# Expert token lists built in three groups instead of two, and expert 0's first layer run between the last group's sums

## The reference

```python
route_prob = jax.nn.softmax(xf @ Ws + bs, axis=-1).T
route_vals, routes = jax.lax.top_k(route_prob, k)      # E = 8 experts, k = 512 tokens each
xin = xf[routes]
h = jax.nn.gelu(jnp.einsum('ekd,edf->ekf', xin, W1) + b1[:, None, :])     # D = 256, F = 1024
out = jnp.einsum('ekf,efd->ekd', h, W2) + b2[:, None, :]
out = out * route_vals[..., None]
final = jnp.zeros((N, D)).at[routes.reshape(-1)].add(out.reshape(-1, D))
```

## Time and profile before

| what | us |
|---|---|
| median of 3 runs | 802.96 |
| lowest, highest | 799.78, 806.54 |
| span of the profiled execution (first to last instruction) | 760.2 |
| TensorE busy in the span | 695.7 |
| VectorE busy | 501.5 |
| ScalarE busy | 348.2 |
| GpSimd busy | 247.4 |

### The profile page before, as it was taken

One profiled execution on the slowest core, in us unless ns is written; L12 is line 12 of the kernel. 1 busy time (PEld: TensorE's weight loads), 2 busy tenths in 40 slices (PEclk: granted clock), 3 DMA queues, 4 the chain that ended last, 5 costly groups with the idle time before them and its releaser, 6 DMA issues.

```text
span 760.2 us, 25608 instructions
## 1 busy us (share of the span) xinstructions
PE 695.7 (92%) x11058; PEld 618.6 (81%) x11058; DVE 501.5 (66%) x1159; ACT 348.2 (46%) x765; POOL 247.4 (33%) x358
## 2 busy tenths in 40 slices
PE   7998998999989999999999999508999999999993
PEld 6886787989978999899899888407689998999992
DVE  6716774555446678777767677678378878877820
ACT  2663544445544546655656564530353345325410
POOL 5510044555644413223140431001734253203333
PEclk9998999999999999999999998755899999999997
DMA  7960024343443635454544453720735255312213
GB/s 201 391 276 2 31 99 153 109 135 124 157 149 112 196 96 158 135 165 140 168 109 142 138 164 108 262 49 3 233 130 154 54 156 139 120 21 28 29 21 36
DMA packets 75467, 96.81 MB, mean 127 GB/s; under 512 B 11337, under 2 KB 67057, under 8 KB 74202
## 3 DMA queue, kind: packets, MB, share of 16 engines
q1 hardware_dynamic: 62250, 69.52, 28.0%
q0 software_dynamic: 12288, 25.12, 13.2%
q10 hardware_dynamic: 816, 0.53, 0.2%
HBM read 53.78 MB, written 41.55 MB: 125 GB/s over the span
## 4 chain that ended last, share of the span: by engine, by line
PE 78%; DVE 10%; issue 4%; DMA 3%; POOL 2%; ACT 1%; POOLq 0%; DVEq 0%
PE bank L1828 41%; PE attn L1828 27%; PE bank L1786 3%; PE bank L1880 2%; DVE arena L1488 2%; PE bank L1887 1%; DMA arena<-x_p,idxs 1%; PE attn L2189 1%; DMA big<-o_m,gidx 1%; DVE st L1043 1%; PE attn L1771 1%; PE attn L1990 1%; POOL arena L524 1%; POOL big L467 1%; DVE big L1056 1%
## 5 line engine op out<-in xcount | busy, mean ns | idle before, releaser
L1828 PE MATMUL attn<-arena 32*32 32x64 f32 (+4 forms) x6048 | 140.3, 225 | 9.2 <-issue 7.3
L1828 PE MATMUL bank<-xT,arena 128*128 128x128 f32 (+2 forms) x964 | 145.8, 306 | 0.0
L1828 PEld LDWEIGHTS attn<-arena 32*32 32x32 f32 (+3 forms) x6048 | 114.2, 120 | 33.2 <-issue 15.4
L1828 PEld LDWEIGHTS bank<-xT,arena 128*128 128x128 f32 x964 | 124.3, 192 | 11.2 <-issue 5.8
L467 POOL DMA_INDIRECT big<-o_m,gidx x64 | 71.0, 1109 | 159.7 <-PE bank L1828 116.9
L460 POOL DMA_INDIRECT x_c<-big,sidx x64 | 68.6, 1071 | 119.3 <-PE bank L1828 88.9
L1828 PE MATMUL bank<-arena,xT 128*128 128x128 f32 (+2 forms) x640 | 107.1, 320 | 0.1
L1828 PEld LDWEIGHTS bank<-arena,xT 128*128 128x128 f32 x640 | 90.0, 199 | 8.6 <-issue 2.9
L543 POOL DMA_INDIRECT out_dram<-arena,idxs x32 | 50.2, 1569 | 109.6 <-ACT arena L1010 99.3
L1165 DVE COPY_PREDICATED arena<-causal,attn 128x1024 f32<-128x1024 int32 x24 | 31.6, 1316 | 71.2 <-PE attn L1828 71.2
L524 POOL DMA_INDIRECT arena<-x_p,idxs x32 | 34.3, 1070 | 98.8 <-DVE idxs L1567 70.8
(11 more groups left out here) (305 smaller groups left out, 1249.2 us busy)
## 6 DMA issues: line engine op xcount, KB each, us to landing
x_c<-zeros SPq DMA_DIRECT2D x8, 1024.0 KB, 9.2
xT<-x_c SPq DMA_DIRECT2D x16, 512.0 KB, 4.1
o_m<-arena SPq DMA_DIRECT2D x16, 512.0 KB, 4.0
xT<-in_L_ffn_W_dram SPq DMA_DIRECT2D x8, 1024.0 KB, 7.9
gs<-in_L_ffn_W_dram SPq DMA_DIRECT2D x8, 1024.0 KB, 7.6
xT<-in_L_attn_x_dram SPq DMA_DIRECT2D x8, 512.0 KB, 5.2
out_dram<-xT SPq DMA_DIRECT2D x8, 512.0 KB, 5.2
arena<-in_L_attn_x_dram SPq DMA_DIRECT2D x7, 512.0 KB, 6.2
```

The costliest lines, as they stand in the source:

```text
L1828: return nc.tensor.matmul(out_, l, r, start=a, stop=z, skip_group_check=True)
```

## The change

The groups become expert 0 alone, experts 1 to 3, and experts 4 to 7. `one_hots` is split, so that the low digit's code of the next group is written before VectorE turns to the wait for the sums of the group before (`low_hots`). The list sums use bank 3, bank 2 and bank 3. Expert 0's blocks move from banks 2 to 5 to banks 4 to 7. The two halves of the last group's sums, and its `spread`, move into `first_hidden`, between the halves of expert 0's layer 1. SP's weights of experts 2 and 3 wait for the last list sum (`s_idx`) and no longer for the turned rows. `warm(14)` and `warm(8)` stand around the second group's sums; the fill-in of 8 behind the last sum goes, and the one of 6 becomes 4. The instructions of POOL are the same as before; `gather(1)` now waits for the second list.

The diff:

```diff
--- before.py
+++ after.py
@@ -34,7 +34,8 @@
 GATED = 1360.0
 E, F = 8, 1024
 HI, LO = 32, 16
-LISTS = ((0, 4), (4, 8))
+LISTS = ((0, 1), (1, 4), (4, 8))
+LIST_BANK = (3, 2, 3)
 NL = len(LISTS)
 PARTS = ((0, NT - 2), (NT - 2, NT))
 EG = max(hi - lo for lo, hi in LISTS)
@@ -666,7 +667,7 @@
 
             def load_w(e):
                 if e == 2:
-                    sp.wait_ge(e_tp, 2)
+                    sp.wait_ge(s_idx, NL)
                 if e >= NW:
                     sp.wait_ge(y_p, 7 * (e - NW + 1))
                 sp.dma_start(w1s[e % NW], W1[e].rearrange("(k p) f -> p k f", p=P)).then_inc(e_w[e % NW], 16)
@@ -968,7 +969,7 @@
             def first_slot():
                 for f in range(FT):
                     act.wait_ge(e_h, f + 1)
-                    nc.scalar.activation(ht[:, 0, f, :], bank[2 + f % 4][:, :], ACT.Gelu_apprx_tanh,
+                    nc.scalar.activation(ht[:, 0, f, :], bank[4 + f % 4][:, :], ACT.Gelu_apprx_tanh,
                                          bias=b1c[:, f:f + 1]).then_inc(e_gl, 1)
                     if f == 2:
                         rows_t(1, 1)
@@ -1545,11 +1546,15 @@
             def over_c(a, lo, hi, n, at):
                 return et(a)[:, lo:hi, at].unsqueeze(2).to_broadcast([P, hi - lo, n, NT // 2])
 
-            def one_hots(q, h):
+            def low_hots(q, h):
                 lo, hi = LISTS[q]
                 at = slice(NT // 2 * h, NT // 2 * h + NT // 2)
                 nc.vector.tensor_tensor(ohb[:, lo:hi, :, at], over_c(digit_f[:, 1, :], lo, hi, LO, at),
                                         over_e(number[:, 0:LO, at], hi - lo), ALU.is_equal).then_inc(s_low, 1)
+
+            def one_hots(q, h):
+                lo, hi = LISTS[q]
+                at = slice(NT // 2 * h, NT // 2 * h + NT // 2)
                 nc.vector.tensor_tensor(oha[:, lo:hi, :, at], over_c(digit_f[:, 0, :], lo, hi, HI, at),
                                         over_e(number[:, :, at], hi - lo), ALU.is_equal)
                 dve.wait_ge(s_low, 2 * q + h + 1)
@@ -1559,7 +1564,8 @@
             def by_digits(q):
                 n = LISTS[q][1] - LISTS[q][0]
                 dve.wait_ge(s_idx, q + 1)
-                nc.vector.tensor_copy(cidx[0:n * HI, q, 0:n * LO], bank[3 + q][0:n * HI, 0:n * LO]).then_inc(s_idxc, 1)
+                nc.vector.tensor_copy(cidx[0:n * HI, q, 0:n * LO], bank[LIST_BANK[q]][0:n * HI, 0:n * LO])\
+                    .then_inc(s_idxc, 1)
 
             def token_list(q):
                 lo, hi = LISTS[q]
@@ -1567,14 +1573,23 @@
                 nc.vector.tensor_scalar(idxs[:, lo:hi, :], attn[:, 0:hi - lo, 8 * q:8 * q + JT], float(B * S // 2),
                                         None, ALU.add).then_inc(s_list, 1)
 
-            for q in range(NL):
-                for h in range(2):
-                    one_hots(q, h)
-                    if q and h == 0:
-                        by_digits(q - 1)
-                        token_list(q - 1)
-            by_digits(NL - 1)
-            token_list(NL - 1)
+            for h in range(2):
+                low_hots(0, h)
+                one_hots(0, h)
+            low_hots(1, 0)
+            by_digits(0)
+            token_list(0)
+            one_hots(1, 0)
+            low_hots(1, 1)
+            one_hots(1, 1)
+            low_hots(2, 0)
+            by_digits(1)
+            token_list(1)
+            one_hots(2, 0)
+            low_hots(2, 1)
+            one_hots(2, 1)
+            by_digits(2)
+            token_list(2)
 
 
             def gate_column(e):
@@ -2155,7 +2170,7 @@
                 n = hi - lo
                 pe.wait_ge(s_oh, 2 * q + h + 1)
                 for t in range(NT // 2 * h, NT // 2 * h + NT // 2):
-                    ins = mm(bank[3 + q][0:n * HI, 0:n * LO], oha[:, lo:hi, :, t].rearrange("p e c -> p (e c)"),
+                    ins = mm(bank[LIST_BANK[q]][0:n * HI, 0:n * LO], oha[:, lo:hi, :, t].rearrange("p e c -> p (e c)"),
                              ohb[:, lo:hi, :, t].rearrange("p e c -> p (e c)"), t == 0, t == NT - 1)
                 if h:
                     ins.then_inc(s_idx, 1)
@@ -2173,10 +2188,10 @@
             by_lists(0, 0)
             by_lists(0, 1)
             spread(0)
+            warm(14, bank[5])
             by_lists(1, 0)
-            warm(5, bank[7])
+            warm(8, bank[5])
             by_lists(1, 1)
-            warm(8, bank[7])
 
             def rows_t(e):
                 pe.wait_ge(e_x[e % 3], 16 * JT * (e // 3 + (e % 3 > 0)))
@@ -2201,7 +2216,7 @@
             def hidden_half(f, h):
                 t = slice(KTOP // 2 * h, KTOP // 2 * h + KTOP // 2)
                 for k in range(2):
-                    ins = mm(bank[2 + f][:, t], w1s[0][:, k, P * f:P * f + P], xet[:, 0, k, t], k == 0, k == 1)
+                    ins = mm(bank[4 + f][:, t], w1s[0][:, k, P * f:P * f + P], xet[:, 0, k, t], k == 0, k == 1)
                 if h:
                     ins.then_inc(e_h, 1)
 
@@ -2209,22 +2224,26 @@
                 pe.wait_ge(e_w[0], 32)
                 first_rows_t(0)
                 spread(1)
-                warm(6, bank[5])
-                pe.wait_ge(s_list, NL)
+                warm(4, bank[5])
                 pe.wait_ge(e_xt, 1)
                 hidden_half(0, 0)
                 hidden_half(1, 0)
+                by_lists(2, 0)
                 first_rows_t(1)
                 hidden_half(2, 0)
+                by_lists(2, 1)
+                pe.wait_ge(e_xt, 2)
                 hidden_half(3, 0)
-                pe.wait_ge(e_xt, 2)
-                for f in range(4):
+                hidden_half(0, 1)
+                spread(2)
+                for f in range(1, 4):
                     hidden_half(f, 1)
+                pe.wait_ge(s_list, NL)
                 rows_t(1)
                 for f in range(4, FT):
                     pe.wait_ge(e_gl, f - 3)
                     for k in range(2):
-                        ins = mm(bank[2 + f % 4][:, :], w1s[0][:, k, P * f:P * f + P], xet[:, 0, k, :], k == 0, k == 1)
+                        ins = mm(bank[4 + f % 4][:, :], w1s[0][:, k, P * f:P * f + P], xet[:, 0, k, :], k == 0, k == 1)
                     ins.then_inc(e_h, 1)
 
             def hidden_product(n, k, w, x, first=True):
@@ -2251,13 +2270,9 @@
                 hidden_product(n, 1, w1sum[:, 2, :], xsum[:, 2, :])
                 if n:
                     pe.wait_ge(h_c, 3 * n)
-                else:
-                    pe.wait_ge(e_gl, 5)
                 hidden_product(n, 2, w1sum[:, 0, :], xsum[:, 0, :])
                 pe.wait_ge(h_u, 2 * n + 1)
                 hidden_product(n, 0, w1_part(e, 0, 1), x_part(e, 1, 0), False)
-                if n == 0:
-                    pe.wait_ge(e_gl, 6)
                 hidden_product(n, 3, w1_part(e, 1, 1), xsum[:, 3, :])
                 pe.wait_ge(h_c, 3 * n + 1)
                 hidden_product(n, 2, w1sum[:, 3, :], x_part(e, 1, 1), False)
```

## The result

| | median us | lowest, highest | runs |
|---|---|---|---|
| before | 799.76 | 792.39, 806.54 | 20 |
| after | 794.41 | 791.82, 800.09 | 20 |

The ratio is 0.9946, with a 95% interval of 0.9928 to 0.9965: a gain of about half a per cent, within 1% as forecast, but with an interval that does not hold 1, where I had said "no shift". The forecast was set on the median of 3 runs, 802.96, and that lies 3.2 us above the median of 20; the other 5.35 us of the miss are the change.

A forecast was written before the change was run, and what follows sets the result against it. The start of hidden(0) was taken to bound the kernel, with expert 1's gather only 1.1 us late. The steps summed to expert 1's turning at 546.4 against 546.40, no shift: 803.0 us, range 799.0 to 808.0.

The forecast's parts named there:

- no shift: Main case: expert 1's turning stays at 546.4 against 546.40, so the time stays 803.0; chance 0.35.
- step 7: Expert 0's first blocks start 1.95 us after the turning, at 533.5; the pair takes 3.03, to 536.5.
- Steps 1 and 2: List 0's codes are ready at 522.2; its 32 sums start at 522.75, take 1.6 us, end at 524.35.
- Steps 3 and 4: Index tile 0 comes at 525.3, 3.4 us earlier; POOL starts at 526.2; expert 0's rows are turned from 531.55.
- step 4: Expert 0's first rows land 4.95 us after the first issue, plus 0.4 for busy VectorE; turning starts at 531.55.
- Step 5: List 1's sums run from 526.7 to near 530.7, ahead of the first turning at 531.55; tile 1 at 533.45.
- Step 6: Expert 1's gather waits for tile 1 until 534.3, lands near 541.3 instead of 546.36; SP's weights start after it.
- Steps 7 and 8: Expert 0's blocks start at 533.5, with list 2's halves of 1.98 us in between; expert 1's turning at 546.4.
- The clock falls in the list sums: Rival: list 2's sums between the blocks keep TensorE at half clock, up to 4.5 us; 805.5, worst 807.5; chance 0.3.
- Small products cost as much as large ones: Rival: list 0's sums take 4.3 us, moving all later steps by 2.7, to 805.7; chance 0.1.
- GpSimd is held up: Rival: GpSimd's first issue waits for VectorE's codes until 529.0, first rows 1.7 us later, 804.7; chance 0.1.
- A gain: Rival: clock up before the first blocks (1.3), list 0's sums 0.4 us (1.2), no overlap cost (0.4); 800.1; chance 0.15.

The follow-up runs named there:

- b_again: The kernel before, unchanged, run and profiled again at the upper level: 799.27 us, ratio 0.9995 to the kernel before.
- a_again2: The changed kernel, unchanged, run a third time, at the lower level: 766.47 us, ratio 1.0026 to the kernel before.
- a_wide: The changed kernel with the second group's products over experts 0 to 3 (128 weight columns, not 96): 763.04 us, ratio 0.9999 to the kernel before.
- b_gather_late: The kernel before with expert 1's gather waiting for the last list: 768.06 us, ratio 1.0046 to the kernel before.
- b_banks4: Fourth run of the kernel before with expert 0's blocks in banks 4 to 7 and the s_list wait behind them: 764.31 us, ratio 0.9991.
- b_banks: The kernel before with expert 0's blocks in banks 4 to 7 and the s_list wait behind them: 763.89 us, ratio 1.0001.
- b_banks2: Second run of the kernel before with expert 0's blocks in banks 4 to 7 and the s_list wait behind them: 764.96 us, ratio 1.0019.
- b_banks3: Third run of the kernel before with expert 0's blocks in banks 4 to 7 and the s_list wait behind them: 763.29 us, ratio 0.9993.
- b_banks_wait_kept: The kernel before with expert 0's blocks in banks 4 to 7 but the s_list wait left ahead of them: 764.65 us, ratio 0.9993.
- b_banks_tile_late: b_banks with VectorE writing the last index tile only after expert 1's rows landed: 764.38 us, ratio 0.9980 to the kernel before.
- b_tile_late: The kernel before with VectorE writing the last index tile only after expert 1's rows landed: 769.36 us, ratio 1.0082.
- b_weights_late: The kernel before with SP's weights of experts 2 and 3 waiting until expert 1's rows are turned: 799.19 us, ratio 0.9991.
- a_again: The changed kernel, unchanged, run again at the upper level: 794.35 us, ratio 0.9926 to the kernel before.
- a_sums_ahead: The changed kernel with both halves of the last list's sums ahead of expert 0's blocks: 797.48 us, ratio 0.9974 to the kernel before.

## Why the prediction was wrong, point by point

**What bounds the kernel now.** "Whatever moves the start of `hidden(0)` moves the end": right. From there to the end of the span are 205.94 to 206.10 us in 19 of the 20 profiles, and 206.80 in b_again. What failed is what follows it: that the gather is late by 1.1 us and that this is all that can be given back, and with it step 7, which lets the blocks start 1.95 us after the turning before the change as well as after it. Both are true of the execution that I read and not of the runs that were timed. There the kernel before starts its blocks 7.18 us after the turning, 5.05 of them idle in the wait `s_list` for the last index tile, and the change, which has this wait behind the blocks, starts them 1.76 after it. So the term that the sum puts at nothing without a reason is the wait `s_list`. What hid it is the step from the profiled span to the median: 42.8 us between them is more than 5% of the time, and I wrote it off.

**Steps 1 and 2, list 0.** The sums start when the 40 fill-ins end, as said, but the fill-ins are not fixed at 3.87 us: they took 3.09 in the profile after, and the sums start 1.19 us after the first code where 2.1 were forecast. The sums take 1.99 for 32 products of 32x16: 0.062 each, 1.6 forecast, within its bounds. The Trainium skill (TensorE: Matmul & The Clock Gate, LDWEIGHTS) has a weight load cost its columns divided by 1.2, in ns, which makes 27 ns here and, as an estimate, 0.85 for the group; the trace's 1.99 is for the whole products and more than twice that, so the loads alone don't set it by that rule.

**Steps 3 and 4.** Index tile 0 is written 3.90 us after the first code (4.42 in a_again2; 4.65 forecast), and the first issue 0.87 behind it takes 1.34, as forecast. The landing of expert 0's rows no longer sets the first turning: there is no wait for a transfer ahead of it in these traces, and a_wide turns them 9.90 us after the first code, so they land at least 1.0 before the 10.9 of step 4.

**Step 5, list 1: the mis-sized term.** The step has 4.0 us for both halves and the fill-in of 8 between them; they took 6.07 (561.16 to 567.23). I had let 16 products of 96x48 cost less than 16 of 128x64, 2.16, with no row for it, and they cost 2.83 and 2.77. So TensorE's own queue, and not the landing of the rows, sets the first turning: 11.36 us after the first code in the profile after and 11.89 in a_again2, where 10.9 were forecast. a_wide puts it at 9.90. The Trainium skill (TensorE: Matmul & The Clock Gate, Weight-path perf modes) has weights load faster when they are 128 columns wide and not fp32; the trace agrees, 2.83 us for 96 columns and 2.15 for 128. I had not used that rule.

**Step 6, the gather.** Expert 1's gathers are issued from 569.67 to 575.85, SP starts the weights at 577.98, and TensorE goes into expert 1's turning without a wait for a transfer. Right, and b_gather_late shows the price of the opposite. That the weights hold up the last gather where they start on top of it, as the step says of the kernel before, is borne out by the variants at the lower level. Where SP starts them 19.5 us after the first code, VectorE's wait for these rows ends at 25.7 (the profile before) or 25.6 (b_banks4); where it starts them at 20.1 to 20.3, at 22.8 to 23.3 (b_banks, b_banks2, b_banks3, b_banks_wait_kept); and with the weights at 18.9 (b_banks_tile_late) it ends at 24.6, with the weights at 25.9 (b_tile_late) at 21.7. So the 1.1 us of wait in the one profile that I read hang on when the weights start, and four of these six executions with the tile on time don't have them. As in the profile before, two issues with VectorE at work beside them are longer, 1.23 and 2.04 where 1.00 is usual.

**Steps 7 and 8, the blocks and list 2.** The pair takes 3.57 to the next row (568.99 to 572.56) where 3.03 was forecast; in the other profiles of these kernels it is between 2.45 and 3.58. From the first block to expert 1's turning are 13.57 (13.60 in a_again2), 12.9 forecast. In the changed kernel at the lower level the whole comes to 27.25 from first code to turning and 34.99 to `hidden(0)`, against 25.75 and 33.55 forecast and seen before: +1.44, of which 0.99 stands ahead of the first turning (step 5) and 0.55 in the pair of blocks (step 7); the rest cancels within 0.2. That is 0.19% of the time, within the interval of a_again2's 0.26%. "No shift" was too good by one microsecond and a half at that level, and too bad by 3.5 at the other.

**The rivals.** *The clock falls in the list sums*: it did not. The granted clock in the profile after (columns of a window: its length, then busy us and count of PE, PEld, DVE, ACT and POOL, granted clock, DMA share, GB/s):

```profile
571.00:572.00 1.00, 1.00 (x4) 0.82 (x3) 1.00 (x2) 0.00 (x0) 0.80 (x1) 0.50 0.37 76
572.00:573.00 1.00, 1.00 (x6) 0.65 (x6) 0.97 (x2) 0.00 (x0) 1.00 (x1) 0.72 0.15 59
573.00:574.00 1.00, 1.00 (x10) 1.00 (x9) 0.00 (x0) 0.00 (x0) 0.69 (x2) 1.00 0.12 21
574.00:581.00 7.00, 7.00 (x75) 6.24 (x74) 0.23 (x1) 1.29 (x2) 5.09 (x6) 1.00 0.52 141
```

It reaches full speed (2.4 GHz) behind the first pair of blocks, while the first half of list 2 runs, and stays there through both halves. *Small products cost as much as large ones*: no for 32 columns, but yes, and more, for 96, which I had not asked. *GpSimd is held up*: the first issue, which the rival is about, took 1.34; another took 2.04, off the path. *A gain*: its chance of 0.15 was for the clock, list 0 and the overlap; the gain came from none of these. The mechanism that decided is one that I did not write down: the wait for `s_list` ahead of the blocks, moved behind them by the change, which costs nothing as long as the tile is on time. I costed the waits `e_gl` at nothing because TensorE shows no idle time there, and said nothing of the wait for `s_list`, for which that profile shows none either.

## What to carry to other kernels

Set the span of a profile against the times of the runs before anything is read from it: if several per cent lie between them, the profile shows another kind of execution, and a wait that costs nothing in it may be the one that the timed runs pay for. A wait that guards only a bank belongs as late in the queue as the bank allows; moving it, with the blocks in other banks, cost nothing where its signal was prompt and saved 0.7 to 0.8% where it was made late. When a group is cut into smaller ones, price the new shape of the weights by a row of its own: 32 columns were cheaper than 128, but 96 were not.

## What the runs showed of the hardware

**Signals that come late.** At the upper level VectorE has waits for which the profile knows no releaser. In the waits of b_again (engine, what and line; released by; us in total, times, longest):

```profile
DVE l L1291 <- remote: 13.8, 4, 3.5
...
DVE idxs L1567 <- remote: 8.0, 1, 8.0
```

The waits of the profile before, of b_banks and of a_again2 have no such line. The first line is four waits in the attention. The late tiles have GpSimd in common. Its last issue of a run of issues, in b_again:

```profile
570.92 1.00 POOL L524 DMA_INDIRECT arena<-x_p,idxs  x1 [0.30 <-issue]
```

The tile was written at 573.00, 1.1 us after that issue ended; 1.1 in b_weights_late, 0.9 in the profile after and in a_again, 0.0 in a_sums_ahead, 0.9 for the wait in b_again's attention that ended at 383.00. The second tile of the profile after, at 568.72, falls in a pause of GpSimd and is on time. It looks as if VectorE got TensorE's signals only when GpSimd pauses between indirect transfers. But the same traces speak against so plain a rule. In b_again VectorE copied the second group's sums at 564.79, 0.05 us after their last product by the profile, in the middle of one of these issues:

```profile
564.79 0.22 DVE L1562 COPY cidx<-bank 128x64 f32<-128x64 f32 x1 [2.27 <-issue]
```

```profile
564.39 1.00 POOL L524 DMA_INDIRECT arena<-x_p,idxs  x1 [0.30 <-issue]
```

The same copy is on time in the profile after (577.99, with an issue from 577.84 on) and in a_sums_ahead (576.33, with one from 575.95 on). So some signals pass amid a run of issues, and others wait until its end or about 1 us more; ScalarE too idles for 1.96 us beside the late tile of the profile after, until 582.37. Why is open, and that GpSimd is the cause was not tested: the kernel with the gather moved away was tried four times and always at the lower level, where the same issues hold up nothing.

**The two levels themselves.** In b_again the first code comes at 552.15, 31.5 us later than in the profile before, with 13.8 of them in the four waits above. As said under the result, the level went with the chip: 14 at the upper one, 9, 10 and 15 at the lower. Only one chip is on record at the upper level, and each series ran at its own time, so whether it is the chip or something else that held for a whole series is not told apart. What makes up the rest of the 31.5 us stays open too.

**Weights of 96 columns.** 2.83 us for 16 fp16 products with 96 columns of weights and 48 moving, 2.15 with 128 and 64, 1.99 for 32 with 32 and 16: 0.177, 0.134 and 0.062 each. The middle width is the dearest. Weights and moving side changed together in all three, so the runs don't tell their shares apart.
